# A four-layer graph network on one core: the constants of the dense stage leave GpSimd, and its ReLU rows move to ScalarE

## The reference, cut to what matters

```python
x2 = x + relu(b_ffn)                          # layer 1 without edges
x3 = x2 + relu(relu(ln(x2)) @ W0 + b0) @ W1 + b1
r  = relu(ln(x3)) @ Wf + bf + bo              # layer 3: skip projection
x4 = x3 + ln(r) * gamma + (r + beta)
```

## Time and profile before

| what | value |
|---|---|
| median of 3 runs | 6727.01 us (6725.3 to 6734.1) |
| the profiled execution's own time | 6730.3 us |
| its span from first to last instruction | 6728.5 us |
| busy in the span | PE 75%, PEld 39%, DVE 73%, ACT 34%, POOL 73% |
| the dense stage in it | from 166 us to 1299 us |
| mean granted TensorE clock | 0.744 of full speed |

### The profile page before, as it was taken

The page is one execution under the profiler, slowest core; times in us unless marked ns, Lnnn a source line. Parts: engine busy times, 40 slices in busy tenths (PEclk is TensorE's granted clock), DMA queues, the critical chain, the costliest instruction groups (busy, mean ns, idle before and its releaser), DMA issues. The chain is left out here.

```text
span 6728.5 us, 70067 instructions
## 1 busy us (share of the span) xinstructions
PE 5032.8 (75%) x17065; PEld 2608.6 (39%) x17065; DVE 4925.5 (73%) x7942; ACT 2275.3 (34%) x5856; POOL 4927.1 (73%) x5468
## 2 busy tenths in 40 slices
PE   0777777588888886888887888555578878788787
PEld 0455555344444442333334444122233334444443
DVE  4899999766676666999996666565567757666666
ACT  0555555322222222433332333121122223333333
POOL 1777777688888883666667887887677757777777
PEclk9877777799999997888885555555578867666666
DMA  9222222233333333555543333344455542222221
GB/s 350 88 95 95 95 95 95 78 75 78 74 79 74 78 75 81 142 145 143 145 130 83 83 82 77 93 109 102 100 136 144 146 119 62 65 65 65 62 61 42
DMA packets 788906, 673.39 MB, mean 100 GB/s; under 512 B 514176, under 2 KB 520906, under 8 KB 788376
## 3 DMA queue, kind: packets, MB, share of 16 engines
q1 hardware_dynamic: 486456, 459.62, 23.5%
q0 software_dynamic: 102464, 90.84, 8.5%
q10 hardware_dynamic: 199584, 118.45, 5.7%
HBM read 396.20 MB, written 276.35 MB: 100 GB/s over the span
## 5 line engine op out<-in xcount | busy, mean ns | idle before, releaser
L736 POOL DMA_INDIRECT sc_xg<-t,keep_gather x792 | 910.7, 1150 | 165.4 <-issue 146.4
L1222 POOL DMA_INDIRECT df_hs<-u,keep_idx x396 | 512.3, 1294 | 129.2 <-issue 108.3
L1222 POOL DMA_INDIRECT hd_gat<-u,keep_idx x396 | 478.5, 1208 | 161.6 <-issue 119.6
L1755 POOL DMA_INDIRECT out_x<-hd_x,keep_scat_out x396 | 458.1, 1157 | 151.4 <-issue 125.4
L1222 POOL DMA_INDIRECT ml_gat<-u,keep_idx x396 | 403.8, 1020 | 168.3 <-issue 70.0
L523 POOL DMA_INDIRECT t<-keep_ptr_pay,keep_scat_ptr x396 | 441.0, 1114 | 108.3 <-issue 106.1
L1222 POOL DMA_INDIRECT pr_gat<-sd,keep_idxsd x396 | 412.5, 1042 | 130.7 <-issue 69.4
L1198 PE MATMUL at_ps_m<-at_vx,keep_weights 128*64 128x512 f32 x792 | 447.3, 718 | 26.0 <-POOL at_vx L1095 26.0
L688 PE MATMUL den_ps_m<-keep_weights,den_hid 128*128 128x64 f32 x1584 | 243.8, 318 | 207.9 <-ACT den_hid L644 207.9
L876 PE MATMUL sc_ps_q<-sc_ht,keep_weights 128*128 128x512 f32 x396 | 272.7, 827 | 140.1 <-issue 84.9
L882 PE MATMUL sc_ps_r<-sc_qx,keep_weights 128*64 128x512 f32 x792 | 376.0, 619 | 1.0 <-DVE sc_prod L799 1.0
(11 more groups left out here) (291 smaller groups left out, 13804.1 us busy)
## 6 DMA issues: line engine op xcount, KB each, us to landing
u<-den_h SPq DMA_DIRECT2D x198, 256.0 KB
t<-tab_row ACTq DMA_DIRECT2D x99, 272.0 KB, 11.3
tab_x<-in_x SPq DMA_DIRECT2D x99, 256.0 KB
den_x<-in_x SPq DMA_DIRECT2D x99, 256.0 KB
out_x<-den_x SPq DMA_DIRECT2D x99, 256.0 KB, 2.6
sc_et<-in_etype_row SPq DMA_DIRECT2D x99, 256.0 KB
at_v<-vt SPq DMA_DIRECT2D x198, 128.0 KB
at_et<-in_etype_row SPq DMA_DIRECT2D x99, 256.0 KB
```

The lines of the kernel that those rows point to most:

```text
L736: pool.indirect_dma_start(xg[i][:, u, :], None, e.T0, bass.IndirectOffsetOnAxis(ap=e.gather0[:, b.n, u:u + 1], axis=0), bounds_check=NP - ...
L1222: pool.indirect_dma_start(gat[i][:, u, :], None, table, bass.IndirectOffsetOnAxis(ap=idx_all[:, c:c + 1], axis=0), bounds_check=rows - 1, ...
L1755: pool.indirect_dma_start(e.out, bass.IndirectOffsetOnAxis(ap=e.scat_out[:, c:c + 1], axis=0), x4[i][:, u, :], None, bounds_check=NP - 1, ...
```

## The change

In `tables`, two more `tensor_copy` operations on DVE write `bias_h`, one partition of 4 x 2 x 64 values (512), with `bfo_cent` and `bfo_beta` side by side. In `dense`:

- POOL computes nothing any more; only the four scatters per step stay, and they wait for `x2_done` of the step before.
- `x2` and `x2b` are computed by DVE.
- The two constants of the projection are no longer added by elementwise operations (`n4.cent` and `x3b` are gone). PE adds them: ahead of the two `wf2` matmuls of each PSUM bank comes a matmul with one row of `ones` (K = 1) and `bias_h`, 512 columns, which starts the accumulation.
- `h2` and `h3` are no longer one DVE operation each; ACT computes each as eight operations over 128x64 with `rstd` as the scale operand (`scale_rows`).
- The squares of norm 2 are one ACT operation, and DVE sums them (as the other two norms already do).
- The hidden layer is two PSUM tiles and two ACT operations of 512 instead of one of 1024.
- The order of the work in a step is new on every engine, in four parts.

The diff, cut to its core:

```diff
+                for half, bias in ((0, e.bfo_cent), (1, e.bfo_beta)):
+                    link(v.tensor_copy(e.bias_h[0:1, :, half, :], bias[0:1, :].unsqueeze(1).broadcast_to([1, TU, D])))
...
+    def vector(self, v, st, part):
+        e, d, f, g = self.e, st, st.back(2), st.back(4)
+        n2, n3, n4 = self.n2, self.n3, self.n4
+        if part == 0:
+            if self.on(f):
+                v.wait_ge(self.m_ready, f.n + 1)
+                v.wait_ge(self.x2b_done, f.n + 1)
+                wait(v, self.hx_done, f.n - (U - 1))
+                v.tensor_tensor(self.x3[f.s][:, :, :], self.ps_m[:, :, :], self.x2b[f.s][:, :, :], ALU.add).then_inc(self.x3_done, 1)
+            if self.on(g):
+                n4.sumsq(v, g)
+            if self.on(f):
+                v.wait_ge(self.x3_done, f.n + 1)
+                n3.total(v, self.x3[f.s][:, :, :]).then_inc(n3.chain, 1)
+            if self.on(d):
+                v.wait_ge(self.x_in[d.s], 16 * (d.k + 1))
+                v.tensor_tensor(self.x2[:, :, :], self.xin[d.s][:, :, :], self.rows(e.relu_b[:, :]), ALU.add).then_inc(self.x2_done, 1)
+        if part == 1:
+            if self.on(f):
+                v.wait_ge(n3.chain, 2 * f.n + 1)
+                wait(v, self.h3_done, f.n)
+                n3.shift(v, self.x3[f.s][:, :, :])
+            if self.on(g):
+                v.wait_ge(self.h_ready, g.n + 1)
+                wait(v, self.x4_done, g.n)
+                v.tensor_tensor(self.hx[:, :, :], self.ps_h[:, :, 1, :], self.x3[g.s][:, :, :], ALU.add).then_inc(self.hx_done, 1)
+                v.wait_ge(n4.rooted, g.n + 1)
+                v.reciprocal(n4.rstd[:, :], n4.std[:, :]).then_inc(n4.chain, 1)
+            if self.on(d):
+                v.wait_ge(self.x2_done, d.n + 1)
+                n2.total(v, self.x2[:, :, :]).then_inc(n2.chain, 1)
+            if self.on(g):
+                v.wait_ge(n4.chain, g.n + 1)
+                v.tensor_tensor(self.f1[:, :, :], self.ps_h[:, :, 0, :], n4.over(n4.rstd), ALU.mult).then_inc(self.f1_done, 1)
+        if part == 2:
+            if self.on(f):
+                n3.sumsq(v, f)
+            if self.on(d):
+                wait(v, self.x3_done, d.n - (U - 1))
+                v.tensor_tensor(self.x2b[d.s][:, :, :], self.x2[:, :, :], self.rows(e.W["b1_row"]), ALU.add).then_inc(self.x2b_done, 1)
+                v.wait_ge(n2.chain, 2 * d.n + 1)
+                wait(v, self.h2_done, d.n)
+                n2.shift(v, self.x2[:, :, :])
+            if self.on(f):
+                v.wait_ge(n3.rooted, f.n + 1)
+                v.reciprocal(n3.rstd[:, :], n3.std[:, :]).then_inc(n3.chain, 1)
+        if part == 3:
+            if self.on(g):
+                v.wait_ge(self.f1_done, g.n + 1)
+                v.tensor_tensor(self.f1[:, :, :], self.f1[:, :, :], self.rows(e.W["gamma"]), ALU.mult).then_inc(self.g1_done, 1)
+            if self.on(d):
+                n2.sumsq(v, d)
+            if self.on(g):
...
+                v.tensor_tensor(self.x4[g.s][:, :, :], self.f1[:, :, :], self.hx[:, :, :], ALU.add).then_inc(self.x4_done, 1)
+            if self.on(d):
+                v.wait_ge(n2.rooted, d.n + 1)
+                v.reciprocal(n2.rstd[:, :], n2.std[:, :]).then_inc(n2.chain, 1)
+
+    def scalar(self, a, st, part):
+        e, d, f, g, d1, f1 = self.e, st, st.back(2), st.back(4), st.back(1), st.back(3)
...
+        def scale_rows(n, h, b, out, done):
+            a.wait_ge(n.chain, 2 * b.n + 2)
+            wait(a, out[b.s], 16 * b.k)
+            for j in range(RN):
+                m = a.activation(h[b.s][:, j, :], n.cent[:, j, :], ACT.Relu, scale=n.rstd[:, j:j + 1])
+            m.then_inc(done, 1)
+
+        if part == 0:
+            if self.on(g):
+                a.wait_ge(self.h_ready, g.n + 1)
+                wait(a, self.n4.summed, g.n)
+                a.activation(self.n4.sq[:, :, :], self.ps_h[:, :, 0, :], ACT.Square).then_inc(self.n4.squared, 1)
+                self.n4.root(a, g, eps)
+        if part == 1:
+            if self.on(f):
+                self.n3.square(a, f)
+            if self.on(d1):
+                a.wait_ge(self.t2, d1.n + 1)
+                a.copy(self.h2t[:, :], self.ps_t2[:, :]).then_inc(self.t2_kept, 1)
+            if self.on(f1):
+                a.wait_ge(self.t3, f1.n + 1)
+                a.copy(self.h3t[:, :], self.ps_t3[:, :]).then_inc(self.t3_kept, 1)
+        if part == 2:
+            if self.on(f):
+                self.n3.root(a, f, eps)
+            if self.on(d1):
+                for half in range(2):
+                    a.wait_ge(self.hid_ready, 2 * d1.n + half + 1)
+                    a.activation(self.hid[:, half, :], self.ps_hid[half][:, :], ACT.Relu, bias=e.W["b0"]).then_inc(self.hid_kept, 1)
+            if self.on(d):
+                self.n2.square(a, d)
+        if part == 3:
+            if self.on(f):
+                scale_rows(self.n3, self.h3, f, self.h3_out, self.h3_done)
+            if self.on(d):
+                self.n2.root(a, d, eps)
+                scale_rows(self.n2, self.h2, d, self.h2_out, self.h2_done)
...
+                turn(self.ps_t2, self.h2[d.s]).then_inc(self.t2, 1)
...
+                turn(self.ps_t3, self.h3[f.s]).then_inc(self.t3, 1)
+        if part == 2:
+            if self.on(d):
+                wait(pe, self.t2_kept, d.n + 1, passed)
+                for half in range(2):
...
+                    pe.matmul(self.ps_hid[half][:, :], e.W["w0"][64 * half:64 * half + 64, :],
+                              self.h2t[64 * half:64 * half + 64, :], start=True, stop=True).then_inc(self.hid_ready, 1)
+            if self.on(f):
+                wait(pe, self.t3_kept, f.n + 1, passed)
+                wait(pe, self.hx_done, f.n, passed)
+                wait(pe, self.f1_done, f.n, passed)
+                for bank in range(2):
+                    pe.matmul(self.ps_h[:, 4 * bank:4 * bank + 4, :, :], e.C["ones"][0:1, :], self.e.bias_h[0:1, :, :, :],
+                              start=True, stop=False, skip_group_check=True)
+                    for c in (2 * bank, 2 * bank + 1):
+                        m = pe.matmul(self.ps_h[:, 2 * c:2 * c + 2, :, :], self.h3t[:, c * P:(c + 1) * P],
+                                      e.W["wf2"], start=False, stop=(c % 2 == 1), skip_group_check=True)
+                m.then_inc(self.h_ready, 1)
+        if part == 3:
+            if self.on(d):
+                wait(pe, self.hid_kept, 2 * d.n + 2, passed)
+                wait(pe, self.x3_done, d.n, passed)
+                for j in range(RN):
...
+                m.then_inc(self.m_ready, 1)
...
+                for n in range(count):
+
+                    wait(pool, den.x2_done, n, e.pool_passed)
+                    for c in range(CH * n // count, CH * (n + 1) // count):
+                        pool.indirect_dma_start(pairs, bass.IndirectOffsetOnAxis(ap=e.scat_ptr[:, c:c + 1], axis=0),
```

More of the change, by code:

```diff
@@ L294, in build @@
         tables(nc, e, dst_row, chunk_id, edge_id, src_idx, dst_idx, node_type, consts, weights)
-        dense(nc, e)
+        dense(nc, e, NG)
         scores(nc, e)
@@ L484, in dense @@
+def dense(nc, e, count):
     with ExitStack() as ctx:
         s = Scope(nc, ctx, "den")
[L486 to L500, removed]
@@ L501, in dense @@
-        t3, t3_kept, h_ready = [s.sem(n) for n in ("t3", "t3k", "hr")]
-        ptr_out = s.sems("ptr_out")
-        rows = lambda b: b.unsqueeze(1).broadcast_to([P, RN, D])
+        den = Dense(s, e, 0, count)
+        ptr_out = s.sem("ptr_out")
         with nc.Block() as block:
@@ L508, in _ @@
                 pairs = e.T0.rearrange("n (a b) -> (n a) b", b=2)
[L510 to L530, removed]
@@ L535, in _ @@
+                wait(pool, ptr_out, 16 * CH, e.pool_passed)
             @block.sync
             def _(sp):
[L537 to L556, removed]
+                for n in range(count + 6):
+                    den.sync(sp, den.step(n))
+                den.sync_end(sp)
             @block.vector
             def _(v):
[L560 to L595, removed]
-                    if d.on():
-                        v.wait_ge(n2.rooted, d.n + 1)
-                        cd.put(v.reciprocal(n2.rstd[:, :], n2.std[:, :]))
-                    if f.on():
-                        n3.sumsq(v, f)
-                    if d.on():
-                        cd.join()
-                        wait(v, h2_out[d.s], 16 * d.k)
-                        n2.relu_to(v, h2[d.s][:, :, :]).then_inc(h2_done, 1)
-                        cd.end()
-                    if f.on():
-                        v.wait_ge(n3.rooted, f.n + 1)
-                        cf.put(v.reciprocal(n3.rstd[:, :], n3.std[:, :]))
-                    if g.on():
-                        cg.join()
-                        v.wait_ge(hx_done, g.n + 1)
-                        wait(v, x4_out[g.s], 16 * g.k)
-                        v.tensor_tensor(x4[g.s][:, :, :], f1[:, :, :], hx[:, :, :], ALU.add).then_inc(x4_done, 1)
```

(47 more changed lines are left out.)

121 lines of the change are left out of this document (85 added, 36 removed).

## The result

The kernel after takes 7342.02 us (median of 4 runs, 7330.95 to 7348.18), the kernel before 6726.16 us beside it: ratio 1.0912, interval 1.0893 to 1.0931. It is slower by 616 us; forecast were 195, and 7090 was the end of the range.

A forecast was written before the change was run, and what follows sets the result against it. DVE was taken to bound the dense stage at 11.11 us per step; afterwards a ring through PE would set 13.1 us. (13.1 - 11.11) x 98 = +195 us gave 6922 us, range 6770 to 7090.

The forecast's parts named there:

- 14 operations at 0.60 us: DVE in a dense step: 14 large operations before and after, with three reciprocals 8.73 us.
- the hold of 2.07 us: DVE in a dense step: two operations held while POOL computes, 2.07 us together, gone after the change.
- The rings: Dense stage: two loops of engines waiting for each other, closing once per step, forecast at 11.9 and 13.1 us.
- B: Loop through DVE, ACT and PE, ending with the second product that gives the next x3: 13.1 us, the longer ring.
- the part outside PE: DVE and ACT work before PE in loop B: 4.20 us and three handovers of 0.04, 4.32 us.
- ACT's rows: 16 scale_rows operations over 128x64 per dense step on ACT: 339 ns each, starting every 0.24 us.
- A: Loop between DVE and ACT via the square of norm 4: 11.9 us; as the deciding ring a rival, 20%.
- So rows don't count: PE: one-row matmuls cost as much as 128-row ones, so the pair was priced as a second projection, 2.47 us.
- the projection and the one-row pair stay at their mean: PE in loop B: both keep the kernel before's mean of mixed clocks, 2 x 2.47 us.
- the second product at 2.00: PE in loop B: it follows the projection with no gap, so its short time of 2.00 us was taken.
- The rival "half clock": PE at 1.2 GHz, with only transposes for 4.3 us per ring: loop B 16.6 us, +538, 7265 us; chance 7%.
- most second products still take 2.00: Argument against half clock: in the kernel before, with pauses of 2 us and more, most take 2.00 us.

The follow-up runs named there:

- The version with both changes: The kernel after with bf16 constants over 128 rows and another operation order on DVE and ACT: ratio 0.9714 to the kernel before, step 9.16 us.
- without the constants: The kernel after without the two one-row matmuls, so the output lacks the projection's constants: ratio 1.0193 to the kernel before, step 12.31 us.
- With 128 rows: The kernel after with its two constant matmuls over 128 rows, 127 of them zero, instead of one: ratio 1.0391 to the kernel before, step 13.60 us.
- the new order: The kernel after, one-row matmuls kept, with transposes copied before squares, hidden halves before rows, and DVE's independent work interleaved: ratio 1.0271, step 12.83 us.

## Why the prediction was wrong

- *DVE's side was right.* 14 operations at 0.60 us (a price that stands in the earlier trace rows; the comparison with eight ACT rows puts it in the earlier trace rows), the hold of 2.07 us gone (L154 at 685 ns), no scatter that holds anyone. The version with both changes shows that this is worth 2 us per step where nothing else decides (9.16 against 11.16). In the kernel after DVE is 50% busy and not near 70%, since the step is longer than forecast.
- *The rings were right.* B decides, DVE's wait ends with the second product, and the part outside PE measured 4.29 us against 4.32. ACT's rows cost what was forecast, and did not matter while B decided. A is the next ring: 12.31 us measured without the constants, against 11.9.
- *The time of a one-row matmul at a given clock was right as far as its own record goes*: 2.07 us for 512 columns, as much as 2.07 for the same columns over 128 rows. "So rows don't count" left out what the change of rows does to the group behind it: 4.01 us against 3.57 for a constant matmul and a projection half.
- *The clock was wrong, and this is the step that failed*: "the projection and the one-row pair stay at their mean", and the second product at 2.00. I took the mixture of clocks from the kernel before as a property of the stage. The one-row matmuls and the pause of the ring changed it: 13.41 us on PE instead of 8.78. With 128 rows the step is 13.60, near the 13.1 forecast, so of the 4.3 us that were missed the rows explain 3.8, an estimated 2.9 by the clock and 0.9 by the later starts. That 13.60 comes so near 13.1 is in part luck: the projection and the constants were not at their mean there either, but at 1.2 GHz up to the first half of the projection and at 2.4 GHz behind it. The loss can't be booked to the rows alone: the new order, with the one-row matmuls kept, takes 4.6 us off the same step. How many rows between 1 and 128 it takes, and why one row does not lift the clock, stays open.
- *The rival "half clock"* had the mechanism on PE but 16.6 us and a chance of 7%. Its price was short by 0.8 us. In the step shown, PE's part was 13.41 us and not 12.29: the four groups of the projection and the constants take 909.37 - 901.49 = 7.88 us and not twice 3.39, and most of that is the later start behind a group with another number of rows. The argument against it ("most second products still take 2.00") held for a kernel with no one-row matmul in it.
- *The row count.* The Trainium skill, in TensorE: Matmul & The Clock Gate, Why this matters for your kernels, says that K=32 takes the time of K=128. The record of one row agrees at equal clock (2.07 and 2.07 us), the start of the next group does not. The Trainium skill, in Part 1 of the same page, says that activity releases the throttle. Measured here, the busy share of PE does not tell the clock: 98% busy went with 0.65 (one row), 85% with 0.83 (128 rows).

## What to carry to other kernels

Before work is moved to TensorE, ask what it does to TensorE's clock as well as what it costs at today's: in this kernel a matmul over one row took the time of one over 128 and took the others' speed with it. So where a constant is accumulated by matmul, try it over all 128 rows, and in bf16 parts if it must be cheap, and look at the granted clock of the stage. When queues are rewritten by hand, look for rings that close once per step; freeing the busiest engine gains nothing while the longest ring of the new queues is longer than the old step.

## What the runs showed that was not expected

- One row against 128 rows, all else equal: granted clock 0.52 and 0.74 in the kernel after (step 17.43 and 13.60 us), 0.65 and 0.83 in the kernel before (12.42 and 11.16 us).
- A PE that is 98% busy with one-row matmuls among the rest ran at a mean clock of 0.65; the fastest version ran at 0.97 with PE 70% busy.
- The pause alone does not hold the clock down: from the second product to the next hidden pair it takes 4.29 us in the kernel after (clock 0.52), 4.31 with 128 rows (0.74), and 5.72 in the step shown without constants (0.76).
- The same kernel before took 6726, 6610, 6613 and 6692 us (medians) on the chips used, while the step of its dense stage with the 128-row matmuls added was 11.16 us as in the first. What follows the last `x3` took 5446.9 us in the first and 6611.5 - 1281.0 = 5330.5 us in that run, so the difference between those two lies outside the dense stage.
